# A convolution-and-experts block: another order of statistics and powers in phase 1, and normalisation and copies on other engines in phase 2

## The chip, the cores and the metric

The kernel runs on one core of a Trainium2 chip. Its engines are TensorE (PE, matmuls; PEld are its weight loads), VectorE (DVE), ScalarE (ACT), GpSimd (POOL) and the DMA queues of SyncE (SP) and GpSimd. Each engine executes its own instructions in program order, and engines wait for each other through semaphores. The metric is the device time of one execution in microseconds (us). PEclk is the TensorE clock that was granted, as a share of full speed; it has two levels, 1.0 (2.4 GHz) and 0.5 (1.2 GHz).

## The reference

```python
x = x + conv(ln_c(x))          # x: 16 x 56 x 56 tokens of 96 channels, f32
t = t + ffn(ln_t(t))           # t: the same 50,176 tokens

def conv(x):                   # 7x7 windows, 49 steps each
    w = ln(x, ln1_w, ln1_b)
    h[k] = w[k] @ Bm + h[k-1] @ A;   xr = h @ Cm
    return xr + gelu(ln(xr, ln2_w, ln2_b) @ W1 + b1) @ W2 + b2

def ffn(x):                    # 4 experts, the best 2 are kept
    probs = softmax(x @ gate_w + gate_b)
    masked = probs * top2mask / (sum(kept probs) + 1e-9)
    return sum_e masked[e] * (gelu(x @ w1[e] + b1[e]) @ w2[e] + b2[e])
```

The reciprocal standard deviations of the normalisations are the powers (var + eps) ** -0.5, and the softmax needs e ** (score - best score). Both are computed on GpSimd.

## The kernel before

**Phase 1** (the function `periods`, 49 tiles of 1,024 tokens) computes the convolution part of all tokens, the gate scores and the position of each token in a list sorted by its pair of experts, and scatters the rows to HBM by indirect DMAs of GpSimd (`scatter`, line 451, 8 for a tile). The tiles are the 49 steps of the recurrence; each has two halves of 512 tokens. Work on several tiles is interleaved in a period p. With r = p + 1, a period holds:

- TensorE: six `up` units (three 512-column matmuls each, lines 1040 to 1042) and six `down` units (line 1051; units 0 and 3 begin with line 1048, which must wait until VectorE has emptied the bank `tok_ps`) of tile p; `from_state(r)` (line 1075), `from_input(p+3)` (line 1060), transposes `turn_h(p+2)` and `turn_xr(r)` (line 1030), and two tiny `rank` matmuls of tile p-1 (lines 1114 and 1115), which need the finished gate of VectorE.
- VectorE: `take_state`, statistics of the input (`x_in`), of the recurrent rows (`xr`) and of the result rows (line 703 and 707, then `variance`, line 714), `gate`, `shift` (line 854), `add_x2` (lines 739 and 742, which empty `tok_ps`), `positions`, the sum `x_xr` (line 863) and `y_low` (line 754), the low part of a split into two fp32r numbers.
- GpSimd: per period one power of 16 columns (`powers_of_variance`, line 437, for `x_in` of tile p+4 and `xr` of tile r together), one of 8 columns (`rstd_t`, line 442) and the scatters.
- ScalarE: six gelus (line 569), `copy_xr` (line 545), `scale_in` (line 530, and the gate columns in line 533), `normalise_xr` (line 554, needs `shift`), `copy_h` (line 538) and `y_high` (line 562), in this order at a period's end: `normalise_xr(r,0)`, `copy_h` twice, `normalise_xr(r,1)`, `gelu(p,5)`, `scale_in(p+3,1)`, `y_high(r,0)`; `y_high(p,1)` opens the next period.

The chain that leads into the next period is thus: `from_state`, `copy_xr`, statistics, variance, power, `shift`, `normalise_xr`, transposes, `y_high`, `y_low`, first `up`. Regions of PSUM are guarded by `Region.take`: a matmul that writes one waits for the semaphore of its last reader. The input products and the rank matmuls share the region `inp`.

**Phase 2** takes 103 blocks of 512 sorted rows, of one pair of experts each. A block has 6 units u (3 for either expert); unit n = 6b + u has `up2(n)` and `down2(n)` on TensorE (lines 1160 to 1162 and 1174 to 1176), `gelu2` and `part_hi` on ScalarE (lines 610 and 616) and `part_lo` on VectorE (line 915). In step u the engines issue `up2(n+3)`, `gelu2(n+3)`, `part_hi(n+3)`, `part_lo(n+3)` and `down2(n)`. After three units the expert's result y lies in a PSUM bank; `copy_y2` copies it with the bias to SBUF (ScalarE, line 628), TensorE transposes it back (`turn_y2`, line 1183: that of the first expert in step 3, that of the second in step 1 of the next block), and VectorE adds it, weighted, to the rows (`combine`, line 969). VectorE computes the two weights of each row in step 2 (`weights`, lines 928 to 941) from the powers of GpSimd (`powers`, line 474), and `numbers` (line 957) gives the indices. GpSimd issues for each block the powers of the next one and four indirect DMAs that store the result (line 485). `normalise(b+2)` (line 950, VectorE, step 3) makes the normalised rows of a later block, `turn_t` (line 1146) transposes them in step 0, and `t_hi` and `t_lo` split them.

## Time and profile before

| | us |
|---|---|
| median of 3 runs | 2251.65 (2246.73 to 2255.51) |
| the profiled execution | 2249.75, span 2248.0 |
| phase 1, first `up` of tile 0 to first `up` of tile 48 (48 periods) | 65.0 to 1101.0 |
| handover: last tile, table of blocks, first rows | 1101.0 to 1146.2 |
| phase 2, to the end of the last block but for its stores | 1146.2 to 2234.3 |

Busy shares over the span are 90% for PE, 73% for PEld, 70% for DVE, 65% for ACT and 70% for POOL. They are averages over two phases with different limits. The granted clock of TensorE is 0.88 in phase 1 and 0.99 in phase 2. The page's shares of the chain that ended last are 39% POOL, 24% issue, 21% PE and 9% DVE. A timeline row gives the start, the duration, the engine, the line, the operation with out<-in, the shapes and the count, and in brackets the idle time of the engine ahead of it and what ended it; the start of the next row tells how soon the engine went on, since instructions overlap.

### The profile page before, as it was taken

To read this page: it belongs to the slowest core of one execution; us is meant where nothing else is said; L and a number is where in the kernel's file an instruction comes from. 1 tells how busy PE (TensorE), PEld (TensorE's weight loads), DVE (VectorE), ACT (ScalarE), POOL (GpSimd) and SP (SyncE) were. 2 spreads that over 40 slices of the span, in tenths; PEclk is the share of its full clock that TensorE was granted. 3 is DMA by queue.
4 is the path that set the end of the run, shared out by engine and by line. 5 is a ranking of instruction groups with operands and counts; after the bars stand their busy time and mean duration, and the time that the engine had idled before them with its cause. 6 is when DMAs were issued, how large, how long until landed. Compare 5 with 4: busy or idle time off the path is not lost.

```text
span 2248.0 us, 41456 instructions
## 1 busy us (share of the span) xinstructions
PE 2013.8 (90%) x10865; PEld 1643.5 (73%) x10865; DVE 1583.5 (70%) x7089; ACT 1461.7 (65%) x3019; POOL 1581.4 (70%) x1147
## 2 busy tenths in 40 slices
PE   4899999999999898889759999999999999999996
PEld 3788888888888788778637676676676666666664
DVE  5576666666676776676548777777777777777775
ACT  1555555454555555555338888888888888888885
POOL 2265555565555655655638888888898888988887
PEclk9988888888899999999869999999999999999998
DMA  5112122121212212221045555655556556555552
GB/s 156 45 51 60 50 62 58 52 64 46 64 46 64 65 48 64 57 61 29 25 138 177 175 175 166 178 167 171 176 163 178 173 167 178 166 177 174 165 180 68
DMA packets 120249, 251.68 MB, mean 112 GB/s; under 512 B 26689, under 2 KB 43707, under 8 KB 120016
## 3 DMA queue, kind: packets, MB, share of 16 engines
q1 hardware_dynamic: 91168, 207.24, 32.1%
q0 software_dynamic: 25728, 40.00, 5.5%
q10 hardware_dynamic: 3120, 1.80, 0.3%
q8 instruction: 89, 1.46, 0.3%
q14 instruction: 144, 1.18, 0.2%
HBM read 203.91 MB, written 46.00 MB: 111 GB/s over the span
## 4 chain that ended last, share of the span: by engine, by line
POOL 39%; issue 24%; PE 21%; DVE 9%; ACT 3%; another core or an unknown queue 1%; DMA 1%; SPq 1%; POOLq 0%; ACTq 0%; DVEq 0%
POOL out L485 27%; PE tok_ps L1051 7%; POOL rstd L437 6%; POOL ex L474 4%; PE turn_ps L1030 3%; DVE stats L703 3%; PE y_ps L1060 3%; PE mix_ps L1075 2%; POOL sorted_rows L451 2%; DVE moment L707 2%; PE up_ps L1040 1%; PE up_ps L1042 1%; PE up_ps L1041 1%; DVE h_tok L726 1%
## 5 line engine op out<-in xcount | busy, mean ns | idle before, releaser
L485 POOL DMA_INDIRECT out<-out_sb,idx x412 | 613.6, 1489 | 135.8 <-issue 112.4
L451 POOL DMA_INDIRECT sorted_rows<-rows,pos x392 | 384.9, 982 | 110.6 <-issue 108.4
L915 DVE TENSOR_TENSOR g_lo<-g,g_hi 128x512 fp32r<-128x512 f32 x618 | 398.2, 685 | 13.3 <-ACT g_hi L616 12.7
L616 ACT CAST g_hi<-g 128x512 fp32r<-128x512 f32 x618 | 382.2, 618 | 13.1
L1051 PE MATMUL tok_ps<-d_mlp,g 128*128 128x100 f32 x2352 | 360.5, 303 | 3.1 <-issue 3.1
L1051 PEld LDWEIGHTS tok_ps<-d_mlp,g 128*128 128x128 f32 x2352 | 336.9, 219 | 24.5 <-issue 23.5
L474 POOL TENSOR_TENSOR ex<-euler,rows 128x8 f32<-128x8 f32 x206 | 339.7, 1664 | 11.0 <-DMA rows<-sorted_rows 9.8
L569 ACT ACTIVATE g<-up_ps 128x512 f32<-128x512 f32 x294 | 172.9, 596 | 218.5 <-PE up_ps L1042 208.3
L1174 PE MATMUL mix_ps<-g_hi,ew 128*96 128x512 f32 x618 | 252.8, 409 | 65.8 <-issue 35.9
L437 POOL TENSOR_TENSOR rstd<-var_eps,neg_half 128x16 f32<-128x16 f32 x52 | 157.1, 3022 | 163.2 <-issue 97.6
L442 POOL TENSOR_TENSOR rows<-var_eps,neg_half 128x8 f32<-128x8 f32 x49 | 82.3, 1679 | 236.2 <-DVE var_eps L714 236.2
L1175 PE MATMUL mix_ps<-g_hi,ew 128*96 128x512 f32 x618 | 244.3, 395 | 0.0
L1176 PE MATMUL mix_ps<-g_lo,ew 128*96 128x512 f32 x618 | 243.7, 394 | 0.0
L754 DVE TENSOR_TENSOR y_lo<-turn_ps,y_hi 96x512 fp32r<-96x512 f32 x98 | 67.1, 686 | 243.3 <-issue 126.8
L628 ACT ACTIVATE y_sb<-mix_ps,ew 96x512 f32<-96x512 f32 x206 | 141.3, 686 | 112.6 <-PE mix_ps L1176 99.0
L554 ACT ACTIVATE xr_n<-xr,shift,rstd 128x96 f32<-128x96 f32 x392 | 151.8, 462 | 84.7 <-DVE shift L854 84.7
L610 ACT ACTIVATE g<-turn_ps 128x512 f32<-128x512 f32 x310 | 185.2, 597 | 32.5 <-PE turn_ps L1162 19.6
L610 ACT ACTIVATE g<-up_ps 128x512 f32<-128x512 f32 x308 | 183.5, 596 | 33.1 <-PE up_ps L1162 20.8
L1174 PEld LDWEIGHTS mix_ps<-g_hi,ew 128*96 128x96 f32 x618 | 99.5, 161 | 132.6 <-issue 59.5
L928 DVE TENSOR_TENSOR both<-ex,pair_of 128x32 f32<-128x32 f32 x103 | 19.8, 192 | 207.8 <-POOL ex L474 207.8
L1075 PE MATMUL mix_ps<-state_aug,h_t 97*128 97x196 f32 x800 | 156.1, 339 | 2.0 <-DVE gate_sum L731 1.4
L1060 PEld LDWEIGHTS y_ps<-in_w,x_t 96*128 96x128 f32 x784 | 138.0, 250 | 21.2 <-ACT gate_sum L533 6.4
(177 smaller groups left out, 4490.6 us busy)
## 6 DMA issues: line engine op xcount, KB each, us to landing
ew<-expert_w SPq DMA_DIRECT2D x206, 384.0 KB
ew<-expert_w SPq DMA_DIRECT2D x206, 288.5 KB
rows<-sorted_rows SPq DMA_DIRECT2D x103, 206.0 KB
x_in<-in_x SPq DMA_DIRECT2D x49, 384.0 KB
x_t<-in_x_chan SPq DMA_DIRECT2D x49, 384.0 KB
out<-out_sb,idx POOLq DMA_INDIRECT x412
sorted_rows<-rows,pos POOLq DMA_INDIRECT x392
sorted_rows<-pad_rows SPq DMA_DIRECT2D x11, 206.0 KB, 11.8
```

Source lines behind the costliest of these rows:

```text
L437: pool.tensor_tensor(rstd[:, n % 2, :, :], var_eps[:, LN_X:LN_T, :], neg_half[:, :].rearrange("p (k s) -> p k s", k=2), ALU.pow).then_inc( ...
L451: pool.indirect_dma_start(out=sorted_rows[:, :], out_offset=bass.IndirectOffsetOnAxis(ap=pos[:, r, s:s + 1], axis=0), in_=rows[:, r, s, :] ...
L474: pool.tensor_tensor(ex[:, b % 2, s:s + 2, :], euler[:, :].rearrange("p (s e) -> p s e", s=2), rows2[:, b % IN_RING, s:s + 2, COL_BELOW:CO ...
L485: pool.indirect_dma_start(out=out_rows, out_offset=bass.IndirectOffsetOnAxis(ap=idx[:, r, s:s + 1], axis=0), in_=out_sb[:, r, s, :], in_of ...
L610: act.activation(g[:, n % G_RING, :], up_bank(n), ACT.Gelu).then_inc(gelu2_done, 1)
L616: act.copy(g_hi[:, n % PART_RING, :], g[:, n % G_RING, :]).then_inc(hi_done, 1)
L915: dve.tensor_tensor(g_lo[:, n % PART_RING, :], g[:, n % G_RING, :], f(g_hi[:, n % PART_RING, :]), ALU.subtract).then_inc(lo_done, 1)
L1051: ins = pe.matmul(mlp_ps[:, s, :], g[:, n % G_RING, sub(s)], d_mlp[:, k, :], start=False, stop=(k == KB - 1 and s == HALF_SUBS - 1))
L1060: ins = pe.matmul(in_ps[:, s, :], x_t[:, t % XT_RING, sub(HALF_SUBS * h + s)], in_w[:, :], start=True, stop=True)
L1174: pe.matmul(y2_bank(q), hi, g_hi[:, part, :], start=(k == 0), stop=False)
L1175: pe.matmul(y2_bank(q), lo, g_hi[:, part, :], start=False, stop=False)
L1176: pe.matmul(y2_bank(q), hi, g_lo[:, part, :], start=False, stop=(k == KB - 1)).then_inc(down2_done, 1)
```

## The change

In phase 1, GpSimd computes one 16-column power for `x_in` of tile p+3 and the result rows of tile p-1 (`rstd_tokens`) and one of 8 columns for `xr` of tile r (`rstd_of_xr`), between scatters 0 and 1 and scatters 2 to 7 of tile p-2. VectorE takes both halves of the state with their statistics first, moves the statistics of the input to the end of the period, cuts `gate` in two (`gate_compares`, `gate_pairs`), and does `add_x2(p,0)` between them, ahead of `shift`; `positions` runs one period later, and the sum `x_xr` is made in halves (`add_xr`). Both `y_high` and both `y_low` stand at the end of a period. TensorE does the rank matmuls after the last transposes, ahead of `down(p,5)`. The scattered row holds -mean * rstd in place of the mean.

In phase 2, ScalarE normalises rows (`normalise`, four ACTIVATEs after `part_hi(6b+7)`, in step 4) and VectorE copies y with its bias (`copy_y2`, at the start of step 3, and for the second expert of step 0 of the next block). GpSimd computes one power of 16 columns for a block in place of two of 8. TensorE's order in phase 2 is as before.

```diff
-            def powers_of_variance(tx, tr):
-
-                n = rstd_calls(tx, tr)
+            def rstd_tokens(tx):
+
+                n, tt = token_power(tx), tx - 4
+                if tile(tt):
+                    pool.wait_ge(var_ok[LN_T], tt + 1)
                 if tile(tx):
                     pool.wait_ge(var_ok[LN_X], tx + 1)
-                if tile(tr):
-                    pool.wait_ge(var_ok[LN_R], tr + 1)
                 if tile(tx - 2):
                     pool.wait_ge(x_b_ok, 2 * (tx - 2) + 2)
-                if tile(tr - 2):
-                    pool.wait_ge(xr_n_ok, 2 * (tr - 2) + 2)
-                pool.tensor_tensor(rstd[:, n % 2, :, :], var_eps[:, LN_X:LN_T, :], neg_half[:, :].rearrange("p (k s) -> p k s", k=2),
+                if tile(tt - 2):
+                    pool.wait_ge(id_ok, tt - 1)
+                pool.tensor_tensor(rstd[:, n % 2, :, :], var_eps[:, LN_T:LN_R, :], neg_half[:, :].rearrange("p (k s) -> p k s", k=2),
                                    ALU.pow).then_inc(rstd_ok, 1)
 
-            def rstd_t(t):
-                pool.wait_ge(var_ok[LN_T], t + 1)
-                pool.tensor_tensor(rows[:, t % ROW_RING, :, COL_RSTD], var_eps[:, LN_T, :], neg_half[:, 0:SUBS],
-                                   ALU.pow).then_inc(rstd_t_ok, 1)
+            def rstd_of_xr(t):
+                pool.wait_ge(var_ok[LN_R], t + 1)
+                if t >= 2:
+                    pool.wait_ge(xr_n_ok, 2 * (t - 2) + 2)
+                pool.tensor_tensor(rstd_r[:, t % 2, :], var_eps[:, LN_R, :], neg_half[:, 0:SUBS], ALU.pow).then_inc(rstd_r_ok, 1)
...
             for p in periods():
+                if tile(p + 3) or tile(p - 1):
+                    rstd_tokens(p + 3)
                 if tile(p - 2):
-                    scatter(p - 2, (1,))
-                if tile(p - 1):
-                    rstd_t(p - 1)
+                    scatter(p - 2, (0, 1))
+                if tile(p + 1):
+                    rstd_of_xr(p + 1)
                 if tile(p - 2):
-                    scatter(p - 2, (2, 3))
-                if tile(p + 4) or tile(p + 1):
-                    powers_of_variance(p + 4, p + 1)
-                if tile(p - 2):
-                    scatter(p - 2, (4, 5, 6, 7))
-                if tile(p - 1):
-                    scatter(p - 1, (0,))
+                    scatter(p - 2, (2, 3, 4, 5, 6, 7))
 
             def powers(b):
                 pool.wait_ge(rows_loaded[b % IN_RING], 16 * (b // IN_RING + 1))
                 if b >= 2:
                     pool.wait_ge(weight_step, 6 * (b - 2) + 2)
-                for s in range(0, BSUBS, 2):
-                    pool.tensor_tensor(ex[:, b % 2, s:s + 2, :], euler[:, :].rearrange("p (s e) -> p s e", s=2),
-                                       rows2[:, b % IN_RING, s:s + 2, COL_BELOW:COL_MEAN], ALU.pow).then_inc(ex_ok, 1)
+                pool.tensor_tensor(ex[:, b % 2, :, :], euler[:, :].rearrange("p (s e) -> p s e", s=BSUBS),
+                                   rows2[:, b % IN_RING, :, COL_BELOW:COL_SHIFT], ALU.pow).then_inc(ex_ok, 1)
...
             for p in periods():
                 r = p + 1
                 if tile(p):
-                    y_high(p, 1)
                     gelu(p, 0)
                     gelu(p, 1)
                 if tile(r):
...
                 if tile(r):
                     y_high(r, 0)
+                    y_high(r, 1)
...
+            def normalise(b):
+                act.wait_ge(rows_loaded[b % IN_RING], 16 * (b // IN_RING + 1))
+                if b >= 2:
+                    act.wait_ge(t_turned, b - 1)
+                for s in range(BSUBS):
+                    row = rows2[:, b % IN_RING, s, :]
+                    ins = act.activation(t_tok[:, b % 2, s, :], row[:, COL_X2:COL_BELOW], ACT.Identity,
+                                         scale=row[:, COL_RSTD:COL_ID], bias=row[:, COL_SHIFT:COL_RSTD])
+                ins.then_inc(t_tok_ok, 1)
+
+            normalise(0)
             t_hi(0)
             for n in range(AHEAD):
                 gelu2(n)
                 part_hi(n)
+            normalise(1)
             for b in range(BLOCKS):
                 for u in range(UNITS):
                     n = UNITS * b + u
                     if n + AHEAD < UNITS * BLOCKS:
                         gelu2(n + AHEAD)
-                    if u % KB == KB - 1:
-                        copy_y2(n // KB)
                     if n + AHEAD < UNITS * BLOCKS:
                         part_hi(n + AHEAD)
+                    if u == 4 and b + 2 < BLOCKS:
+                        normalise(b + 2)
                     if u == 0 and b + 1 < BLOCKS:
                         t_hi(b + 1)
...
+            def add_xr(t, h):
+                subs = slice(HALF_SUBS * h, HALF_SUBS * (h + 1))
+                if t >= 2:
+                    dve.wait_ge(x2_ok, 2 * (t - 2) + h + 1)
+                dve.tensor_tensor(x_xr[:, t % 2, subs, :], xr[:, subs, :], x_in[:, t % X_RING, subs, :], ALU.add).then_inc(x_xr_ok, 1)
...
-            def gate(t):
+            def gate_compares(t):
...
+            def gate_pairs(t):
...
             for p in periods():
                 r = p + 1
-                if tile(p):
-                    y_low(p, 1)
                 if tile(p - 1):
                     add_x2(p - 1, 1)
                     rows_stats(p - 1, 1)
-                    variance(LN_T, p - 1, (rstd_t_ok, p - 1))
+                    variance(LN_T, p - 1, (rstd_ok, token_power(p + 2) + 1))
+                if tile(p - 2):
+                    positions(p - 2)
                 if tile(r) or r == -1:
                     take_state(r, 0)
+                if tile(r):
+                    xr_stats(r, 0)
+                    add_xr(r, 0)
+                if tile(r) or r == -1:
+                    take_state(r, 1)
+                if tile(r):
+                    xr_stats(r, 1)
+                    variance(LN_R, r, (rstd_r_ok, r))
+                if tile(p - 1):
+                    gate_compares(p - 1)
+                if tile(p):
+                    add_x2(p, 0)
+                if tile(r):
+                    dve.wait_ge(rstd_r_ok, r + 1)
+                    if r >= 1:
+                        dve.wait_ge(xr_n_ok, 2 * (r - 1) + 2)
+                    dve.scalar_tensor_tensor(shift[:, :], in0=moment[:, LN_R, :, 0], scalar=-1.0, in1=rstd_r[:, r % 2, :],
+                                             op0=ALU.mult, op1=ALU.mult).then_inc(shift_ok, 1)
+                if tile(p - 1):
+                    gate_pairs(p - 1)
+                if tile(r):
+                    add_xr(r, 1)
+                if tile(p):
+                    rows_stats(p, 0)
                 if tile(p + 4):
                     t = p + 4
                     dve.wait_ge(x_loaded[t % X_RING], 16 * (t // X_RING + 1))
                     for h in range(2):
                         half_stats(LN_X, t, h, x_in[:, t % X_RING, :, :])
-                    variance(LN_X, t, (rstd_ok, rstd_calls(t - 1, t - 4) + 1))
+                    variance(LN_X, t, (rstd_ok, token_power(t - 1) + 1))
...
                 if tile(r):
-                    xr_stats(r, 0)
-                if tile(r) or r == -1:
-                    take_state(r, 1)
-                if tile(r):
-                    xr_stats(r, 1)
-                    variance(LN_R, r, (rstd_ok, rstd_calls(r + 2, r - 1) + 1))
-                if tile(p - 1):
-                    gate(p - 1)
-                if tile(r):
-                    n = rstd_calls(r + 3, r)
-                    dve.wait_ge(rstd_ok, n + 1)
-                    if r >= 1:
-                        dve.wait_ge(xr_n_ok, 2 * (r - 1) + 2)
-                    dve.scalar_tensor_tensor(shift[:, :], in0=moment[:, LN_R, :, 0], scalar=-1.0, in1=rstd[:, n % 2, LN_R, :],
-                                             op0=ALU.mult, op1=ALU.mult).then_inc(shift_ok, 1)
-                if tile(p):
-                    add_x2(p, 0)
-                if tile(p - 1):
-                    positions(p - 1)
-                if tile(r):
-                    if r >= 2:
-                        dve.wait_ge(x2_ok, 2 * (r - 1))
-                    dve.tensor_tensor(x_xr[:, r % 2, :, :], xr[:, :, :], x_in[:, r % X_RING, :, :], ALU.add).then_inc(x_xr_ok, 1)
-                if tile(p):
-                    rows_stats(p, 0)
-                if tile(r):
                     y_low(r, 0)
+                    y_low(r, 1)
...
-            def normalise(b):
...
+            def copy_y2(q):
+                dve.wait_ge(down2_done, KB * (q + 1))
+                if q >= 2:
+                    dve.wait_ge(y2_turned, q - 1)
+                dve.tensor_scalar(y_sb[:, q % 2, :], y2_bank(q), f(ew[0:C, q % EW_RING, E_B2:E_B2 + 1]), None, ALU.add).then_inc(
+                    y2_copied, 1)
...
             for b in range(BLOCKS):
                 for u in range(UNITS):
                     n = UNITS * b + u
+                    if u == 0 and b >= 1:
+                        copy_y2(2 * b - 1)
+                    if u == 3:
+                        copy_y2(2 * b)
                     if u == 1 and b >= 1:
                         combine(2 * b - 1)
                     if u == 2:
@@ -996,8 +1010,7 @@
                         part_lo(n + AHEAD)
                     if u == 0 and b + 1 < BLOCKS:
                         t_lo(b + 1)
-                    if u == 3 and b + 2 < BLOCKS:
-                        normalise(b + 2)
+            copy_y2(2 * BLOCKS - 1)
...
                     turn_h(p + 2, 1)
+                if tile(p + 3):
+                    from_input(p + 3, 1)
+                if tile(p):
+                    down(p, 3)
+                    up(p, 5)
+                if tile(r):
+                    turn_xr(r, 0)
+                if tile(p):
+                    down(p, 4)
+                if tile(r):
+                    turn_xr(r, 1)
                 if tile(p - 1):
                     inp.take(pe, base_set, p)
                     pe.wait_ge(score_counted, p)
                     pe.matmul(rank_ps[:, 0:TYPES], earlier[:, :], count[:, :, SUBS - 1], start=True, stop=True)
                     pe.matmul(rank_ps[:, TYPES:2 * TYPES], ones[:, :], count[:, :, SUBS - 1], start=True, stop=True).then_inc(
                         ranked, 1)
-                if tile(p):
-                    down(p, 3)
-                    up(p, 5)
-                if tile(p + 3):
-                    from_input(p + 3, 1)
-                if tile(r):
-                    turn_xr(r, 0)
-                if tile(p):
-                    down(p, 4)
-                if tile(r):
-                    turn_xr(r, 1)
                 if tile(p):
                     down(p, 5)```

VectorE in phase 1, from the variance of `xr` (the second half of its statistics is just done) to the emptying of `tok_ps`, before:

```order
L714 TENSOR_SCALAR var_eps<-moment 128x8
L763 TENSOR_TENSOR score<-gate_sum,rows 128x32
...
L780 TENSOR_TENSOR rows<-score,top 128x8x4
L783 TENSOR_REDUCE rank<-beaten 128x32
L785 TENSOR_SCALAR kept<-rank 128x32
...
L797 SCALAR_TENSOR_TENSOR count<-restart,of_pair 128x48
L854 SCALAR_TENSOR_TENSOR shift<-moment,rstd 128x8
L739 TENSOR_TENSOR rows<-tok_ps,x_xr 128x4x96
L742 TENSOR_TENSOR gate_sum<-tok_ps,gate_sum 128x16
```

and the same place in the changed kernel:

```order
L715 TENSOR_SCALAR var_eps<-moment 128x8
L771 TENSOR_TENSOR score<-gate_sum,rstd 128x32
...
L784 TENSOR_TENSOR beaten<-score 128x8x3
L740 TENSOR_TENSOR rows<-tok_ps,x_xr 128x4x96
L743 TENSOR_TENSOR gate_sum<-tok_ps,gate_sum 128x16
L861 SCALAR_TENSOR_TENSOR shift<-moment,rstd_r 128x8
L796 TENSOR_TENSOR rows<-score,top 128x8x4
L799 TENSOR_REDUCE rank<-beaten 128x32
```

The emptying of `tok_ps` has moved ahead of `shift`, and the second half of the gate behind it.

VectorE in phase 2, from the index copy of step 2 of one block to the first weight instruction of the next, before:

```order
L957 CAST idx<-rows 128x4
L915 TENSOR_TENSOR g_lo<-g,g_hi 128x512 x2
L950 TENSOR_SCALAR t_tok<-rows 128x96 x4
L969 SCALAR_TENSOR_TENSOR out_sb<-tok_ps,weight,rows 128x96 x4
L915 TENSOR_TENSOR g_lo<-g,g_hi 128x512 x3
L920 TENSOR_TENSOR y_lo<-y_ps,y_hi 96x512
L969 SCALAR_TENSOR_TENSOR out_sb<-tok_ps,weight,out_sb 128x96 x4
L915 TENSOR_TENSOR g_lo<-g,g_hi 128x512
L928 TENSOR_TENSOR both<-ex,pair_of 128x32
```

and in the changed kernel:

```order
L962 CAST idx<-rows 128x4
L930 TENSOR_TENSOR g_lo<-g,g_hi 128x512
L968 TENSOR_SCALAR y_sb<-mix_ps,ew 96x512
L930 TENSOR_TENSOR g_lo<-g,g_hi 128x512
L981 SCALAR_TENSOR_TENSOR out_sb<-tok_ps,weight,rows 128x96 x4
L930 TENSOR_TENSOR g_lo<-g,g_hi 128x512 x2
L968 TENSOR_SCALAR y_sb<-mix_ps,ew 96x512
L930 TENSOR_TENSOR g_lo<-g,g_hi 128x512
L935 TENSOR_TENSOR y_lo<-y_ps,y_hi 96x512
L981 SCALAR_TENSOR_TENSOR out_sb<-tok_ps,weight,out_sb 128x96 x4
L930 TENSOR_TENSOR g_lo<-g,g_hi 128x512
L943 TENSOR_TENSOR both<-ex,pair_of 128x32
```

The four `t_tok` rows are gone, and a copy of y (`y_sb<-mix_ps,ew`) stands behind the first `g_lo` after the weights and another ahead of the last but one.

## Rows read from the trace of the kernel before

**Rows 1.** Windows: stretch, busy (x) of PE, PEld, DVE, ACT, POOL, PEclk, DMA.
```profile
65.00:1101.00 1036.00, 951.36 (x5717) 853.92 (x5717) 690.43 (x4089) 549.63 (x1419) 585.96 (x465) 0.88 0.19 53
...
1146.20:2234.30 1088.10, 1013.09 (x4944) 749.61 (x4944) 844.23 (x2783) 891.24 (x1545) 949.34 (x614) 0.99 0.57 169
594.74:618.35 23.61, 22.27 (x122) 20.11 (x121) 15.07 (x88) 11.74 (x30) 12.52 (x10) 0.78 0.19 52
704.25:723.65 19.40, 17.70 (x123) 15.77 (x122) 14.49 (x87) 10.93 (x29) 11.86 (x10) 1.00 0.20 47
```

**Rows 2.** Timeline of TensorE in phase 1, in the tile that begins at 704.25.
```profile
709.21 1.49 PE L1075 MATMUL mix_ps<-state_aug,h_t 97*128 97x196 f32 x8
...
716.17 0.36 PE L1114 MATMUL y_ps<-count,earlier 128*128 128x6 f32 x2 [0.52 <-DVE count L797]
...
717.60 0.44 PE L1048 MATMUL tok_ps<-b_parts,ones_r 2*128 2x400 f32 x1 [0.85 <-DVE gate_sum L742]
```

**Rows 3.** Timeline of VectorE in phase 1, the next tile.
```profile
732.64 0.53 DVE L726 TENSOR_TENSOR h_tok<-mix_ps,x_b 128x384 f32<-128x384 f32 x1
...
734.34 0.17 DVE L714 TENSOR_SCALAR var_eps<-moment 128x8 f32<-128x8 f32 x1
...
735.52 0.19 DVE L780 TENSOR_TENSOR rows<-score,top 128x32 f32<-128x32 f32 x1
...
737.70 0.17 DVE L854 SCALAR_TENSOR_TENSOR shift<-moment,rstd 128x8 f32<-128x8 f32 x1 [0.78 <-POOL rstd L437]
...
743.80 0.69 DVE L754 TENSOR_TENSOR y_lo<-turn_ps,y_hi 96x512 fp32r<-96x512 f32 x1 [2.33 <-ACT y_hi L562]
```

**Rows 4.** Timeline of GpSimd in phase 1, the same tile.
```profile
728.81 1.68 POOL L442 TENSOR_TENSOR rows<-var_eps,neg_half 128x8 f32<-128x8 f32 x1 [4.50 <-DVE var_eps L714]
...
734.65 3.01 POOL L437 TENSOR_TENSOR rstd<-var_eps,neg_half 128x16 f32<-128x16 f32 x1 [1.67 <-issue]
```

**Rows 5.** Timeline of ScalarE in phase 1, the same tile.
```profile
725.48 0.58 ACT L562 CAST y_hi<-turn_ps 96x512 fp32r<-96x512 f32 x1 [2.60 <-remote]
...
731.12 0.48 ACT L545 COPY xr<-mix_ps 128x384 f32<-128x384 f32 x1 [0.87 <-PE mix_ps L1075]
...
737.90 1.55 ACT L554 ACTIVATE xr_n<-xr,shift,rstd 128x96 f32<-128x96 f32 x4 [2.10 <-DVE shift L854]
...
743.17 0.60 ACT L562 CAST y_hi<-turn_ps 96x512 fp32r<-96x512 f32 x1
```

**Rows 6.** Timeline of GpSimd in phase 2, one block.
```profile
1599.76 3.29 POOL L474 TENSOR_TENSOR ex<-euler,rows 128x8 f32<-128x8 f32 x2
...
1607.53 2.65 POOL L485 DMA_INDIRECT out<-out_sb,idx  x1 [0.30 <-issue]
1610.18 3.30 POOL L474 TENSOR_TENSOR ex<-euler,rows 128x8 f32<-128x8 f32 x2
```

**Rows 7.** Waits from 1200 to 2200 us: engine, line, waited for, us, times, longest.
```profile
DVE both L928 <- POOL ex L474: 200.6, 96, 2.1
```

**Rows 8.** Timeline of VectorE in an early block of phase 2.
```profile
1174.00 1.00 DVE L969 SCALAR_TENSOR_TENSOR out_sb<-tok_ps,weight,out_sb 128x96 f32<-128x96 f32 x4
...
1175.51 0.19 DVE L928 TENSOR_TENSOR both<-ex,pair_of 128x32 f32<-128x32 f32 x1
...
1176.79 0.69 DVE L915 TENSOR_TENSOR g_lo<-g,g_hi 128x512 fp32r<-128x512 f32 x1
```

**Rows 9.** Timeline of TensorE there: steps 1 and 3, then step 1 again.
```profile
1173.40 0.49 PE L1183 MATMUL tok_ps<-ident,y_sb 96*128 96x96 f32 x4
...
1176.57 0.49 PE L1183 MATMUL tok_ps<-ident,y_sb 96*128 96x96 f32 x4
...
1182.97 0.49 PE L1183 MATMUL tok_ps<-ident,y_sb 96*128 96x96 f32 x4
```

**Rows 10.** Timeline of ScalarE there: the first gelu after the second transposes, and its high part.
```profile
1177.83 0.60 ACT L610 ACTIVATE g<-turn_ps 128x512 f32<-128x512 f32 x1
1178.46 0.63 ACT L616 CAST g_hi<-g 128x512 fp32r<-128x512 f32 x1
```

62 lines of the change are left out of this document (26 added, 36 removed).

## The prediction

> **What bounds the kernel now.** I read the windows first, because the busy shares of the page average two phases with different limits. Phase 1 takes 1036 us for 48 periods, 21.58 each, at a granted clock of 0.88; phase 2 takes 1088 at 0.99 [rows 1]. These two are 94% of the span, so each is priced by itself.
>
> In phase 1 TensorE sets the time, together with its clock. The tile that begins at 704.25 runs at full clock and takes 19.40; the one at 594.74 has a granted clock of 0.78 and takes 23.61 [rows 1]. In the first, TensorE waits twice: 0.52 for the finished gate ahead of the rank matmuls, and 0.85 for the emptying of `tok_ps` ahead of `down(p,3)` [rows 2]. Both waits recur in every tile, and most of them are followed by a stretch at half clock. Without the two waits a tile at full clock has 19.40 - 1.37 = 18.03 of work. The second wait comes from `add_x2`, which stands behind `shift` on VectorE, and `shift` waits for the power of 3.01 us on GpSimd [rows 3, 4].
>
> In phase 2 the waits name GpSimd: VectorE waits 200.6 us, 96 times, for the powers [rows 7]. From one pair of powers to the next pass 10.42 us, and GpSimd goes straight from the last store into the next power [rows 6]. A block is therefore 10.42, although TensorE can do one in 9.57: in an early block, where GpSimd is not yet behind, the same transposes recur after 1182.97 - 1173.40 [rows 9].
>
> **Phase 1, part by part.** Times are counted from the first `up` of a tile at full clock. The second `from_state` ends at 709.21 + 1.49 - 704.25 = 6.45 [rows 2], and the copy of `xr` starts at 6.50 and takes 0.48 [rows 5]. Now the statistics of the input stand in front of what follows on VectorE; they go to the end of the period. So `h_tok` starts at 7.00, the variance 1.70 later (734.34 - 732.64, [rows 3]) and ends at 8.87. The power has 8 columns, which took 1.68, in place of 16 with 3.01 [rows 4]: with 0.1 for the handing over it ends at 10.65, and `shift` starts at 10.70. Beside the power VectorE has the compares (735.52 - 734.34 = 1.18, and 0.1 for one more instruction) and `add_x2` (about 0.55), which fit. `tok_ps` is then empty well before `down(p,3)`, and the rank matmuls stand four units later than the gate needs: both waits go.
>
> What is late next? From `shift` to `y_low` pass 743.80 - 737.70 = 6.10, to the first `up` another 0.69 and 0.06 [rows 3]: the next tile could start at 17.55. ScalarE has `gelu(p,4)` just ahead of `normalise_xr` then, 0.3 more: 17.85. A new wait appears: the rank matmuls share the region `inp` with `from_input(p+3,1)`, so they wait for the last gate columns of ScalarE, copied just ahead of `y_high`, which starts 5.47 after `shift` [rows 5], that is at about 16.5. That leaves 1.5 for rank and `down(p,5)` until 18.0. Chain and work meet: I take 18.03. The power of 16 columns is now for other rows and has several us of slack; the scatters (some 1.27 each) end before the next one is asked for. Cutting `x_xr` in two and one more small instruction cost 0.2 on VectorE, which still has slack ahead of `take_state`. `positions` (about 1.1) fits ahead of the state, which arrives 3.1 after the period's start.
>
> Sum: 48 x (21.58 - 18.03) = 170 less. ScalarE has nine waits of about 2.60 with no releaser in the trace, one of them at 725.48 [rows 5]; the chain has no slack for these, so 9 x 2.6 = 23 comes back: **-147**. If the clock still falls in part of the tiles, a tile costs 19 to 19.5 and the gain is 100; without the 23 it is 170.
>
> **Phase 2, part by part.** GpSimd gains: one power of 16 columns (3.01, [rows 4]) for two of 8 (3.29, [rows 6]), 0.3 a block. That would be the whole story if GpSimd stayed the bound. But `copy_y2` has moved into VectorE's order, behind `combine`, the weights and two `g_lo`, while TensorE's `turn_y2` of step 3 still stands where it stood, ahead of every further `up2`. The loop, from the start of that transposition:
>
> - TensorE transposes, does `up2(6b+7)`, ScalarE its gelu and high part: in the early block from 1176.57 to the start of `g_hi` at 1178.46 [rows 9, 10], 1.89; ScalarE goes on 0.52 later, 2.41.
> - `normalise(b+2)` now stands here. Its nearest row is `xr_n`, four ACTIVATEs of 96 columns out of SBUF with scale and bias per row: 1.55, 1.45 to the next start [rows 5]. On VectorE it took less, but the row to go by is ScalarE's own. 3.86.
> - Gelu and high part of unit 6b+8: 1178.46 + 0.63 - 1177.83 = 1.26 [rows 10]. 5.12, and 0.02 to VectorE.
> - VectorE: `g_lo` 0.60, copy of y 0.66, `g_lo` 0.60, `y_lo` 0.60, `combine` and `g_lo` 1.51 (1175.51 - 1174.00), weights and indices 1.28 (1176.79 - 1175.51), `g_lo` 0.60 [rows 8], copy of y until done 0.74, and 0.06 to TensorE. 5.14 + 6.65 = 11.79.
>
> The trace of before has no copy of y on VectorE; its nearest row is `y_lo`, 96x512 from PSUM, 0.69 [rows 3], and I add 0.05 for the pointer operand (bounds 0.60 and 0.80, so the loop is 11.6 to 11.9). So a block takes **11.79 in place of 10.42**, whatever GpSimd does: +1.37 over 102 blocks is +140. In the early block one sees the same thing: TensorE reaches its transposes of step 3 at 1176.57, when VectorE is still at the weights (until 1176.79), behind which come `g_lo` and then the copy [rows 8, 9].
>
> TensorE then stands still for 11.79 - 9.57 = 2.2 in one piece in every block. In phase 1 waits of 0.52 and 0.85 close together were enough to bring half clock in most tiles [rows 1, 2]. At half clock the transposes and the `up2` at the loop's head (about 1.2) double: +1.2 if that happens in each block, 0 if in none. I take one block in three, +0.4: in phase 2 TensorE is otherwise denser than in phase 1. Sum: (1.37 + 0.4) x 102 = **+180**.
>
> A rule of the Trainium skill bears on ScalarE's new part ("VectorE: DVE Perf Modes", the section on the TRN2 errata): instructions with SBUF sources pay a fixed extra latency each, and ScalarE takes 224 cycles and one per element. Four pieces of 96 columns would be 1.07 us by it, an estimate, and the sum 39 us lower; here the trace's 1.55 is used.
>
> The handover between the phases has the 3.01 power in place of 1.68 and else the same chain: 0 to 3, taken as 0.
>
> **Sum.** 2249.75 (profiled execution; the median is 1.9 higher) - 147 + 180 = **2283**.
>
> **Rivals.**
> 1. The loop holds, but the clock does not fall in phase 2, and phase 1 gets its 147 to 170: 2249.75 - 147 + 140 = 2243, down to 2220. For it: phase 2 is at 0.99 now, with a wait of TensorE in every block. This ends on the fast side where phase 1 gains over 150. Chance 0.28.
> 2. VectorE, freed of its wait of 2.1 for the powers [rows 7], runs ahead far enough, and the copy is never late: TensorE's 9.57 decides, 2249.75 - 147 - 0.85 x 102 = 2016; with GpSimd as the bound at 10.1 it is 2070. Against it stands the loop, in which GpSimd has no part. The Trainium skill supports half of it ("SBUF — State Buffer", Who interferes with whom): a `tensor_scalar` between fp32 tiles in SBUF locks GpSimd out of its port while it makes descriptors, and the `t_tok` rows are such; without them the stores would be shorter. The store of 2.65 [rows 6] starts after them and lies beside `g_lo`, so the trace does not bear the rule out for the longest store. Chance 0.08.
> 3. The clock falls after the wait in nearly each block: 2249.75 - 147 + 2.57 x 102 = 2365. It decides where half clock follows more than two thirds of the waits. Chance 0.14.
> 4. Phase 1 keeps half of its half-clock stretches, because the rank matmuls' new wait (0.5) is followed by little work: 2249.75 - 100 + 180 = 2330. Chance 0.14.
>
> **How the numbers follow.** My forecast, 2262 to 2310 with 2283 in it, has 0.36, of which 0.07 lies within 0.5%. A measurement of this kernel can tell 0.5% (11 us) from no change. Faster by more: 0.19 of rival 1 and 0.08 of rival 2, 0.27. Within: 0.09 of rival 1 and 0.07, 0.16. Slower: 0.57. The range takes in rival 1 with the short loop (2205) and most of rivals 3 and 4 (2380); rival 2 and the worst of rival 3 are left out.
>
> **What would show it.** In the changed profile: no wait ahead of `tok_ps` in phase 1, a wait ahead of the rank matmuls of about 0.5, a period of about 18.0 to 18.6 and a clock near 1.0 there. In phase 2: a wait of about 2 us of TensorE ahead of the transposes of `y_sb` once per block, none of VectorE for the powers, GpSimd waiting for `combine`, and a block of 11.8 to 12.2. A block under 10.42 would refute the loop; a period over 20 the phase 1 part.

## The result

The changed kernel takes **2429.7 us** (2419.9 to 2467.5) beside 2250.4 of the kernel before: a ratio of 1.077, interval 1.073 to 1.082. Slower was right, but 2283 was forecast, in a range up to 2380. Later runs on other chips showed that both kernels take different times there. The record does not name the chip of the result; it is called A here.

| chip | before | changed kernel | ratio [interval] |
|---|---|---|---|
| A (the result) | 2250.4 | 2429.7 | 1.077 [1.073, 1.082] |
| B | 2248.3 | 2377.9 | 1.059 [1.055, 1.063] |
| F | 2177.0 | 2260.1 | 1.037 [1.033, 1.040] |

The execution profiled with the result (2467.5) was a slow one, 45 above the median of the others (2422.5) and left out of the ratio, so the profile of after is read from the run of the unchanged kernel on chip B (`a0_after`), beside the one on chip F (`g0_after`). The windows are phase 1 (first to last `up`) and phase 2 (first to last transposition of y), for the kernel before, the changed kernel on B, and the changed kernel on F. Columns: stretch, busy us of PE, PEld, DVE, ACT, POOL, granted clock, DMA share, GB/s.

```profile
65.00:1110.30 1045.30, 960.57 (x5771) 861.43 (x5772) 697.29 (x4130) 552.62 (x1424) 591.52 (x470) 0.89 0.19 53
1167.00:2232.40 1065.40, 998.72 (x4904) 739.46 (x4902) 834.37 (x2754) 882.21 (x1531) 941.88 (x609) 1.00 0.57 169
```

```profile
68.60:1052.70 984.10, 906.50 (x5767) 795.21 (x5768) 704.69 (x4220) 540.70 (x1424) 599.53 (x467) 0.95 0.19 56
1110.70:2360.40 1249.70, 1073.88 (x4903) 780.46 (x4903) 894.99 (x2555) 911.20 (x1727) 746.91 (x509) 0.94 0.51 144
```

```profile
69.00:937.60 868.60, 852.88 (x5767) 759.51 (x5768) 699.94 (x4220) 539.49 (x1424) 602.29 (x467) 0.99 0.21 64
993.40:2244.50 1251.10, 1075.65 (x4903) 782.60 (x4903) 894.66 (x2554) 911.19 (x1727) 747.12 (x509) 0.94 0.51 144
```

Phase 2 is longer by 184, the same on both chips (1249.7 and 1251.1), and 180 was forecast. Phase 1 is the part that went wrong: on B it gained 61 in place of 147, and on F it is 116 shorter than on B with the same instructions. On A it gained about 17: the profiled execution has 1073.0 for phase 1, less the 45 by which it lay high, an estimate that puts all of the 45 there. Its phase 2 is 1248, no longer than on B, so the 45 do lie ahead of it.

**Phase 2 in the profile.** Transposes of y on TensorE (chip B), with the idle time ahead in brackets; these answer to [rows 9]:

```profile
1612.99 0.55 PE L1196 MATMUL tok_ps<-ident,y_sb 96*128 96x96 f32 x4 [1.46 <-DVE y_sb L968]
...
1619.57 0.55 PE L1196 MATMUL tok_ps<-ident,y_sb 96*128 96x96 f32 x4
...
1624.81 0.55 PE L1196 MATMUL tok_ps<-ident,y_sb 96*128 96x96 f32 x4 [1.88 <-DVE y_sb L968]
```

ScalarE and then VectorE in the same block, in answer to [rows 10] and [rows 8]:

```profile
1614.31 0.60 ACT L606 ACTIVATE g<-turn_ps 128x512 f32<-128x512 f32 x1 [2.20 <-PE turn_ps L1175]
...
1615.47 1.54 ACT L626 ACTIVATE t_tok<-rows 128x96 f32<-128x96 f32 x4
1616.91 0.58 ACT L606 ACTIVATE g<-up_ps 128x512 f32<-128x512 f32 x1
1617.52 0.62 ACT L612 CAST g_hi<-g 128x512 fp32r<-128x512 f32 x1
```

```profile
1618.17 0.69 DVE L930 TENSOR_TENSOR g_lo<-g,g_hi 128x512 fp32r<-128x512 f32 x1 [1.88 <-ACT g_hi L612]
1618.78 0.74 DVE L968 TENSOR_SCALAR y_sb<-mix_ps,ew 96x512 f32<-96x512 f32 x1
...
1622.14 0.18 DVE L943 TENSOR_TENSOR both<-ex,pair_of 128x32 f32<-128x32 f32 x1
...
1623.42 0.68 DVE L930 TENSOR_TENSOR g_lo<-g,g_hi 128x512 fp32r<-128x512 f32 x1
1624.02 0.74 DVE L968 TENSOR_SCALAR y_sb<-mix_ps,ew 96x512 f32<-96x512 f32 x1
```

This is the forecast loop. From the transposes at 1612.99 over ScalarE's rows to `g_lo` at 1618.17 pass 5.18 (5.14 forecast), and from there over `g_lo`, copy, `g_lo`, `y_lo`, `combine`, `g_lo`, weights, `g_lo` and copy to the next transposes 6.64 (6.65 forecast). VectorE has no wait for a power any more, and GpSimd waits for the combination:

```profile
POOL out L481 <- DVE out_sb L981: 343.1, 88, 5.0
```

The wait of TensorE brings half clock in part of the blocks. The block above, and the next one:

```profile
1612.99:1624.81 11.82, 9.94 (x48) 7.16 (x49) 8.70 (x26) 8.88 (x17) 7.48 (x6) 1.00 0.56 152
1624.81:1637.59 12.78, 11.29 (x49) 8.28 (x49) 8.91 (x26) 9.12 (x17) 7.04 (x6) 0.87 0.48 137
```

Of 101 blocks, 58 run at full clock with a mean of 11.81 and 43 have a stretch of half clock and a mean of 12.78: 0.97 more in 43%, or 0.41 a block.

**Phase 1 in the profile.** The same tile end on chip B and on chip F. First B: TensorE's transposes of `xr_n`, then ScalarE's `y_hi`, which reads them.

```profile
781.17 0.60 PE L1043 MATMUL turn_ps<-ident,xr_n 128*96 128x128 f32 x4
781.61 1.03 PE L1064 MATMUL tok_ps<-d_mlp,g 128*128 128x100 f32 x8
782.48 0.60 PE L1043 MATMUL turn_ps<-ident,xr_n 128*96 128x128 f32 x4
```

```profile
783.51 0.58 ACT L558 CAST y_hi<-turn_ps 96x512 fp32r<-96x512 f32 x1 [0.19 <-PE turn_ps L1043]
786.50 0.58 ACT L558 CAST y_hi<-turn_ps 96x512 fp32r<-96x512 f32 x1 [2.40 <-remote]
```

Then chip F:

```profile
713.91 0.60 PE L1043 MATMUL turn_ps<-ident,xr_n 128*96 128x128 f32 x4
...
715.22 0.60 PE L1043 MATMUL turn_ps<-ident,xr_n 128*96 128x128 f32 x4
```

```profile
715.92 1.08 ACT L558 CAST y_hi<-turn_ps 96x512 fp32r<-96x512 f32 x2
```

On F both casts run one behind the other as soon as the second transposes end at 715.82. On B the transposes end at 781.77 and 783.08 by their rows, but the second cast starts at 786.50, 3.4 later, and nothing else holds it: ScalarE is idle for 2.40. Of the two semaphores for which it waits, that of `up(5)` had risen by 781.35; that of the transposes changes at 783.49 and 786.47 in the trace. "remote" is what the profile says when a semaphore changed at a moment at which no instruction ended. In the text below this is a **late signal**. The waits of `y_hi` for them in phase 1, on B, and what follows on TensorE:

```profile
ACT y_hi L558 <- remote: 85.2, 42, 2.8
...
PE mix_ps L1088 <- DVE gate_sum L732: 32.4, 36, 1.2
```

On F there is no wait `<- remote` in phase 1, nor this wait of TensorE. There a tile takes 17.82 to 17.85 in 44 of 48 periods, where 18.03 was forecast. One caution goes with the word late: the profile models the ends of matmuls, so the rows cannot tell whether the signal lags behind the work or the work behind its row. What ScalarE waits for is real in either case.

### The profile page after: what moved, and what is told of

The parts are those of the page before. It is cut to its first block, busy times and chain, and to the rows that moved or that the text cites. A ratio compares the mean times of both kernels' runs of the same rounds, so it can differ in the third digit from the quotient of the medians.

```text
span 2465.7 us, 41499 instructions
## 1 busy us (share of the span) xinstructions
PE 2099.8 (85%) x10865; PEld 1673.4 (68%) x10865; DVE 1652.6 (67%) x6981; ACT 1490.6 (60%) x3225; POOL 1398.9 (57%) x1045
## 3 DMA queue, kind: packets, MB, share of 16 engines
q8 instruction: 89, 1.46, 0.3%
## 4 chain that ended last, share of the span: by engine, by line
issue 28%; DVE 22%; POOL 19%; PE 18%; ACT 8%; POOLq 1%; SPq 0%; DMA 0%; another core or an unknown queue 0%; ACTq 0%; DVEq 0%
POOL sorted_rows L452 13%; DVE g_lo L930 7%; DVE y_sb L968 5%; ACT t_tok L626 4%; DVE out_sb L981 4%; POOL rstd_r L444 3%; PE tok_ps L1196 3%; POOL rstd L437 2%; ACT g L606 2%; PE mix_ps L1187 2%; PE mix_ps L1188 2%; PE mix_ps L1189 2%; ACT g_hi L612 2%; PE turn_ps L1173 1%; PE up_ps L1173 1%
## 5 line engine op out<-in xcount | busy, mean ns | idle before, releaser
L481 POOL DMA_INDIRECT out<-out_sb,idx x412 | 421.1, 1022 | 515.4 <-DVE out_sb L981 406.8
L930 DVE TENSOR_TENSOR g_lo<-g,g_hi 128x512 fp32r<-128x512 f32 x618 | 422.9, 684 | 316.1 <-ACT g_hi L612 237.1
L612 ACT CAST g_hi<-g 128x512 fp32r<-128x512 f32 x618 | 383.0, 620 | 19.6
L565 ACT ACTIVATE g<-up_ps 128x512 f32<-128x512 f32 x294 | 174.1, 597 | 300.6 <-PE up_ps L1055 270.3
L1064 PE MATMUL tok_ps<-d_mlp,g 128*128 128x100 f32 x2352 | 344.5, 293 | 0.7 <-issue 0.5
L470 POOL TENSOR_TENSOR ex<-euler,rows 128x16 f32<-128x16 f32 x103 | 335.2, 3254 | 11.3 <-DMA rows<-sorted_rows 10.2
L1064 PEld LDWEIGHTS tok_ps<-d_mlp,g 128*128 128x128 f32 x2352 | 313.1, 205 | 23.4 <-issue 22.1
L437 POOL TENSOR_TENSOR rstd<-var_eps,neg_half 128x16 f32<-128x16 f32 x53 | 156.7, 2957 | 272.4 <-DVE var_eps L715 272.4
L606 ACT ACTIVATE g<-turn_ps 128x512 f32<-128x512 f32 x310 | 183.8, 593 | 161.5 <-PE turn_ps L1175 133.0
L606 ACT ACTIVATE g<-up_ps 128x512 f32<-128x512 f32 x308 | 182.6, 593 | 156.8 <-PE up_ps L1175 117.5
L1196 PE MATMUL tok_ps<-ident,y_sb 96*128 96x96 f32 x824 | 114.0, 262 | 177.2 <-DVE y_sb L968 166.5
L1196 PEld LDWEIGHTS tok_ps<-ident,y_sb 96*128 96x128 f32 x824 | 80.7, 143 | 258.5 <-DVE y_sb L968 238.1
L1088 PE MATMUL mix_ps<-state_aug,h_t 97*128 97x196 f32 x800 | 196.3, 401 | 13.3 <-DVE gate_sum L732 12.5
L1088 PEld LDWEIGHTS mix_ps<-state_aug,h_t 97*128 97x128 f32 x800 | 182.4, 244 | 32.3 <-issue 19.4
L1053 PE MATMUL up_ps<-y_hi,w_hi 98*128 98x512 f32 x294 | 158.2, 538 | 26.7 <-DVE y_lo L761 14.4
L626 ACT ACTIVATE t_tok<-rows 128x96 f32<-128x96 f32 x412 | 158.6, 456 | 36.6 <-DMA rows<-sorted_rows 36.6
L444 POOL TENSOR_TENSOR rstd_r<-var_eps,neg_half 128x8 f32<-128x8 f32 x49 | 83.3, 1701 | 148.4 <-DVE var_eps L715 148.4
```

What stands on the lines that cost most here:

```text
L470: pool.tensor_tensor(ex[:, b % 2, :, :], euler[:, :].rearrange("p (s e) -> p s e", s=BSUBS), rows2[:, b % IN_RING, :, COL_BELOW:COL_SHIFT] ...
L481: pool.indirect_dma_start(out=out_rows, out_offset=bass.IndirectOffsetOnAxis(ap=idx[:, r, s:s + 1], axis=0), in_=out_sb[:, r, s, :], in_of ...
L606: act.activation(g[:, n % G_RING, :], up_bank(n), ACT.Gelu).then_inc(gelu2_done, 1)
L612: act.copy(g_hi[:, n % PART_RING, :], g[:, n % G_RING, :]).then_inc(hi_done, 1)
L930: dve.tensor_tensor(g_lo[:, n % PART_RING, :], g[:, n % G_RING, :], f(g_hi[:, n % PART_RING, :]), ALU.subtract).then_inc(lo_done, 1)
L1064: ins = pe.matmul(mlp_ps[:, s, :], g[:, n % G_RING, sub(s)], d_mlp[:, k, :], start=False, stop=(k == KB - 1 and s == HALF_SUBS - 1))
```

## The experiments

P1 and P2 are the two stretches defined above. Runs on one chip were made together and share the runs of the kernel before.

| run | chip, before there | us | ratio [interval] | P1 | P2 |
|---|---|---|---|---|---|
| a0_after | B, 2248.3 | 2377.9 | 1.059 [1.055, 1.063] | 984 | 1250 |
| a1_old_phase2 | B | 2200.1 | 0.978 [0.976, 0.981] | 989 | 1069 |
| a4_new_phase2 | B | 2429.1 | 1.081 [1.076, 1.085] | 1037 | 1250 |
| a5_small_loads | B | 2373.5 | 1.057 [1.051, 1.062] | 979 | 1248 |
| a2_copy_on_scalar | C, 2244.8 | 2119.0 | 0.941 [0.935, 0.947] | 991 | 990 |
| a3_norm_on_vector | C | 2273.7 | 1.012 [1.007, 1.017] | 981 | 1150 |
| b5_later_turn | C | 2152.2 | 0.959 [0.953, 0.964] | 984 | 1025 |
| b1_scatters_spread | C | 2376.3 | 1.058 [1.053, 1.063] | 980 | 1249 |
| e1_pause | D, 2178.4 | 2042.1 | 0.936 [0.931, 0.942] | 913 | 988 |
| e2_swap | D | 2000.1 | 0.917 [0.911, 0.922] | 870 | 989 |
| e3_positions | D | 2009.3 | 0.921 [0.916, 0.927] | 881 | 989 |
| e4_swap_positions | D | 2011.6 | 0.923 [0.918, 0.928] | 880 | 988 |
| f0_base | E, 2176.0 | 1994.3 | 0.917 [0.913, 0.920] | 865 | 989 |
| f1_pause | E | 2045.9 | 0.940 [0.937, 0.944] | 912 | 988 |
| f2_swap | E | 1998.2 | 0.918 [0.915, 0.922] | 868 | 989 |
| f3_positions | E | 2009.8 | 0.923 [0.920, 0.927] | 882 | 989 |
| g0_after | F, 2177.0 | 2260.1 | 1.037 [1.033, 1.040] | 869 | 1251 |
| g1_pause | F | 2308.8 | 1.060 [1.056, 1.064] | 916 | 1249 |

### The parts, one by one

The theory was that the phases are independent; the rival that phase 1 had gained as forecast and lost it through phase 2.

> The changed kernel once more, as the control beside the other three: 2420 to 2435. From its profile the difference to the kernel before is to be split: phase 1 (first to last up) +10 to +30 where -147 was forecast, phase 2 about +180 as forecast, the handover under 5.

> New phase 1, old phase 2 (rows normalised on VectorE, y copied on ScalarE, two powers per block; the row holds the shift in place of the mean, so VectorE multiplies and adds). If the two parts add up and the new phase 1 is worth nothing: 2245 to 2285. If phase 1 is worth the 147 that I forecast and only lost it through phase 2 (the clock): 2100 to 2120.

> Old phase 1 (which writes the shift in place of the mean, one small instruction for another), new phase 2 whole. If the loop through the copy of y sets phase 2 alone: +165 to +190, 2415 to 2440, a block of 11.8 to 12.3, TensorE waiting 1.5 to 2 ahead of its transposes of y_sb. If part of the slowdown comes from phase 1: below 2400.

Old phase 2 takes 2200, new phase 2 on the old phase 1 takes 2429: -48 and +181 against the kernel before, and the two together are +133 where the whole change is +130. The parts add up; the rival is out. `a1_old_phase2` itself lies between its two forecasts (2245 to 2285 and 2100 to 2120): its P1 is 56 shorter than that of before, where nothing or 147 had been the alternatives. The block of the old phase 2 is 10.47 and VectorE waits for the powers as in [rows 7]: with two powers, GpSimd is the bound again. The forecasts for the control (2420 to 2435, P1 +10 to +30) missed: I had taken them from chip A, P1 from the disturbed execution there.

### Phase 2: which of its edits

`a2_copy_on_scalar` moves the copy of y back to ScalarE, between gelu and high part (ScalarE's order; in VectorE's the two calls go):

```diff
                         gelu2(n + AHEAD)
+                    if u % KB == KB - 1:
+                        copy_y2(n // KB)
```

> The changed kernel with the copy of y back on ScalarE (between gelu and high part, as before); rows still normalised on ScalarE, one power. The control took 2378 on the last chip and its phase 2 is 180 longer than the old one. If the forecast loop (the copy of y late on VectorE) is the cause: most of the 180 goes, and what is left is ScalarE's own work, 8.65 a block before and 1.5 more for the rows, so a block of 10.4 to 11.0 and 2200 to 2265. If the move of the rows to ScalarE is the cause: 2350 or more.

`a3_norm_on_vector` moves the normalising back (VectorE multiplies and adds the shift). The first two lines are ScalarE's order, the others VectorE's:

```diff
-                    if u == 4 and b + 2 < BLOCKS:
-                        normalise(b + 2)
+                    if u == 3 and b + 2 < BLOCKS:
+                        normalise(b + 2)
```

> The changed kernel with the normalising of the rows back on VectorE; the copy of y still on VectorE, one power. The forecast loop loses its 1.45 of ScalarE and would be 10.3: a block of 10.3 to 10.8 and 2200 to 2260. If the copy's place alone is what costs, whatever ScalarE does beside it: 2330 or more.

`b5_later_turn` leaves all work on its engine and moves two calls by a step, first in TensorE's order, then in VectorE's:

```diff
-                    if u == 3:
+                    if u == 4:
                         turn_y2(2 * b)
...
-                    if u == 4:
+                    if u == 5:
                         combine(2 * b)
```

> The changed kernel with TensorE's first transposition of y in a block one step later (step 4 in place of 3) and the combination that reads it one step later too (5 in place of 4); all work stays on its engine. If TensorE's order closes the loop, the copy now has 1.6 more and is never late: TensorE's wait of 1.5 to 2 goes, a block of 10.1 to 11.0, 2200 to 2290. If an engine is simply full (ScalarE or VectorE), nothing changes: 2365 to 2390.

The loop is confirmed, by the run that moves no work above all: with the transposition a step later a block takes 10.0 in place of 11.8, no block has half clock, and the time is below the forecast of 2200 to 2290. TensorE's idle time ahead of the transposes of y falls to 0.3 a block. The copy back on ScalarE gives 9.67 (P2 shorter by 260, 80 under the kernel before). That was better than I had expected (10.4 to 11.0). I had added 1.5 of ScalarE per block to its 8.65; in a window of one block it is busy for 9.53, and the whole block is bound by TensorE:

```profile
606.10:623.93 17.83, 17.54 (x123) 15.68 (x122) 14.73 (x90) 11.27 (x30) 12.81 (x11) 1.00 0.25 70
1612.00:1621.66 9.66, 9.66 (x50) 7.24 (x49) 7.30 (x23) 9.53 (x21) 7.06 (x6) 1.00 0.60 175
```

(These are a tile and a block of the same kernel on chip E.) The normalising back on VectorE gives 11.22; I had expected 10.3 to 10.8. Taking 1.45 out of the loop shortened it by only 0.6: TensorE still waits, 1.48 in the block that follows.

```profile
1599.93 0.55 PE L1196 MATMUL tok_ps<-ident,y_sb 96*128 96x96 f32 x4 [1.48 <-DVE y_sb L964]
...
1611.16 0.55 PE L1196 MATMUL tok_ps<-ident,y_sb 96*128 96x96 f32 x4 [1.48 <-DVE y_sb L964]
```

The rows that VectorE now normalises itself (1600.40 to 1601.41) are not what is left, since VectorE waits twice behind them:

```profile
1603.93 0.69 DVE L916 TENSOR_TENSOR g_lo<-g,g_hi 128x512 fp32r<-128x512 f32 x1 [0.70 <-ACT g_hi L612]
...
1606.98 0.99 DVE L977 SCALAR_TENSOR_TENSOR out_sb<-tok_ps,weight,out_sb 128x96 f32<-128x96 f32 x4 [0.37 <-PE tok_ps L1196]
```

From the transposes at 1599.93 to this `g_lo` pass 4.00, where 5.18 less 1.44 would be 3.74: ScalarE, freed of the rows, now waits for TensorE's next `up2`. From there to the next transposes pass 7.23 in place of 6.64, most of it because `combine` has caught up with TensorE's transposes of step 1 and waits for them. Other waits took the place of the rows.

So it is the copy behind `combine`, weights and `g_lo` on VectorE, together with TensorE's fixed place for the transposes, that costs; the rows on ScalarE add to it. The same trace bears on a page that the prediction weighed ("SBUF — State Buffer", Who interferes with whom, in the Trainium skill). VectorE's `t_tok` is a `tensor_scalar` between fp32 tiles in SBUF, and a store of GpSimd runs beside it. The first row is VectorE's, the second GpSimd's, which starts 0.03 earlier:

```profile
1611.63 1.09 DVE L951 TENSOR_SCALAR t_tok<-rows 128x96 f32<-128x96 f32 x4
```

```profile
1611.60 1.04 POOL L481 DMA_INDIRECT out<-out_sb,idx  x1 [0.30 <-issue]
```

It takes 1.04, as stores do elsewhere (a mean of 1.04 in this kernel, 1.03 with the rows on ScalarE). Stores that start while such an instruction already runs are in the trace of before: there are 100, and they take 1.01 on average and 1.03 at most. So here the page's rule has no price that shows. The mean store of 1.49 belongs to the two kernels with two powers in a block (before, `a1_old_phase2`); what makes their fourth store 2.65 long [rows 6] was not tried.

### Phase 1: where the signals are late

Two suspects stand beside the late signals in the trace of chip B: the burst of the loads of x, and the train of GpSimd's scatters, whose last one starts 1.9 before the signals come, in tile after tile.

`a5_small_loads` lets every load of x beyond the first of each ring move an eighth of its bytes (the edit shown, and the same for the turned copy of x):

```diff
+                n = TOK // P * C if t < X_RING else C
-                sp.dma_start(x_in[:, t % X_RING, :, :].rearrange("p s c -> p (s c)"), x[t, :, :]).then_inc(
+                sp.dma_start(x_in[:, t % X_RING, :, :].rearrange("p s c -> p (s c)")[:, 0:n], x[t, :, 0:n]).then_inc(
```

> The changed kernel, but all loads of x after the first ones of each ring move an eighth of their bytes (an eighth of the columns; the rest of the buffers keeps old rows, so the result is not the reference's). In the changed profile ScalarE waits 1.3 and then 1.0 ahead of y_hi in nearly each tile, for completion signals of TensorE's transposes that come up to 3 us after the transposes' recorded end, and this falls together with the burst of the two loads of x. If the loads hold the signals back: these waits go, a tile takes 18.0 to 19.0, phase 1 is 100 to 150 shorter and the time 2270 to 2330. If the signals are late for another reason (scatters, instruction fetch, TensorE itself being behind its records): within 15 of the control.

`b1_scatters_spread` issues three of a tile's eight scatters one period later, where GpSimd was idle:

```diff
+                if tile(p - 3):
+                    scatter(p - 3, (5, 6, 7))
                 if tile(p + 3) or tile(p - 1):
                     rstd_tokens(p + 3)
...
-                    scatter(p - 2, (2, 3, 4, 5, 6, 7))
+                    scatter(p - 2, (2, 3, 4))
+            scatter(TILES - 1, (5, 6, 7))
```

> The changed kernel, but the last three of a tile's eight scatters are issued one period later, ahead of the power, where GpSimd was idle for 4.3. In the control TensorE's completion signals of the end of a tile come up to 3.8 late, all at one moment that lies 1.92 to 1.95 after the start of the last scatter of the train, whatever else stands there, and the small loads of the run before changed nothing. If the train of scatters holds the signals back: ScalarE's waits ahead of y_hi (85 in all) shrink to under 30, tiles take 18.0 to 18.6 as they now do where no scatter is in flight, and the time falls by 60 to 110, to 2270 to 2320. If scatters hold back signals wherever they are, the delay moves to the start of the tile: within 20 of the control. If they have no part in it: the same waits ahead of y_hi.

Neither changed anything. The waits of `y_hi`, with small loads (chip B, 85.2 in the control) and then with the scatters spread (chip C, where the three other kernels with this phase 1 have 79.8 to 81.8):

```profile
ACT y_hi L560 <- remote: 79.2, 43, 2.8
```

```profile
ACT y_hi L561 <- remote: 84.6, 40, 2.8
```

Neither the bytes of the loads nor the length of the train makes the signals late; the constant distance to the last scatter is that of a schedule in which everything is in step. What is left is something about TensorE itself, or about what carries its signals. The rows spoke for a row of short instructions: at the end of a tile some forty matmuls follow each other 0.11 apart, and in the four tiles of chip B with the most half clock no signal of these transposes is late. The first row is one of the four. The second row, a tile at full clock right behind another of them, has these signals 1.7 and 3.4 late again, though it takes only 18.12:

```profile
124.33:150.11 25.78, 24.27 (x123) 21.56 (x122) 15.16 (x90) 11.72 (x31) 12.83 (x11) 0.74 0.17 50
603.70:621.82 18.12, 17.52 (x123) 15.67 (x122) 14.53 (x89) 10.90 (x29) 12.34 (x10) 1.00 0.24 65
```

To test this I took `a2_copy_on_scalar` as base and made three edits: a pause of TensorE, an order in which `up(5)` breaks the row, and the positions out of the way of `h_tok`. The pause (TensorE; `g1_pause` has it on the changed kernel itself):

```diff
+                    if tile(p):
+                        pe.wait_ge(gelu_done, UNITS * (p + 1))
                     turn_xr(r, 0)
```

The swap (TensorE):

```diff
                     down(p, 3)
-                    up(p, 5)
                 if tile(r):
                     turn_xr(r, 0)
                 if tile(p):
+                    up(p, 5)
                     down(p, 4)
```

The positions (VectorE; `e4_swap_positions` has both this edit and the swap):

```diff
-                if tile(p - 2):
-                    positions(p - 2)
                 if tile(r) or r == -1:
                     take_state(r, 0)
...
                     add_xr(r, 0)
+                if tile(p - 2):
+                    positions(p - 2)
```

> Base: the changed kernel with the copy of y on ScalarE (2119, phase 1 991). One wait added on TensorE and no work: ahead of the first transposes of xr_n it waits for the gelu of unit 5, which comes about 1.0 later than it now starts them. If TensorE's completion signals are late because too many short instructions (0.11 apart) come in a row without a pause (they are late only at the end of that row, and not in tiles in which TensorE runs at half clock): the pause lets them catch up, ScalarE's waits ahead of y_hi for late signals (82 in all) nearly go, and phase 1 gets no longer, or shorter: 930 to 995, 2060 to 2125. If the signals are late for a reason outside TensorE: the pause comes on top, phase 1 1010 to 1045, 2140 to 2175.

> The same base; in TensorE's order the first transposes of xr_n stand ahead of up(5) in place of behind it, so the three long matmuls of up(5) break the row of short ones and the signal for y_hi has less in front of it. Row theory: the signal of the first transposes comes on time, the waits ahead of y_hi fall to 20 to 50, a tile takes 19 to 19.6, phase 1 910 to 960, 2040 to 2090. Cause outside TensorE: the release at the end of the row stays where it is, phase 1 980 to 995, 2110 to 2125.

> The same base; on VectorE the positions of tile p-2 stand behind the first half of h_tok, its gate columns, statistics and x + xr, in place of ahead of them. TensorE now waits 33 in all (34 times about 1.0) ahead of the second from_state for those gate columns. If it is the positions that are in the way: these waits go and phase 1 is 30 to 50 shorter, 2070 to 2090. If the next wait takes their place (the scatters start 1.2 later, and so does the power for the shift behind two of them): phase 1 980 to 1000, 2110 to 2130.

> Both edits together, to see whether they add up: if they do and each works, phase 1 870 to 930, 2000 to 2060; if the tile is then bound by something else, no better than the better of the two.

These four seemed to confirm everything: no late signal in any, and P1 between 870 and 913 where it had been 991. But all four gained, even the one whose edit had nothing to do with TensorE's order, and the kernel before took 2178 on that chip in place of 2245. Without a control there the runs told nothing, so the base ran beside three of them on one chip, E, where the kernel before again took 2176.

> The changed kernel with the copy of y on ScalarE, as control of the next three. If this chip gives late completion signals as the first ones did: about 2119, phase 1 990, 80 of ScalarE's waits for late signals. If it is like the last chip (before at 2178): few or no late signals, phase 1 880 to 930 and about 2010 to 2050, since then the forecast 18.0 per tile and 0.7 to 1.0 of wait behind the positions decide.

> The pause of TensorE ahead of the transposes of xr_n once more, now beside its control. With late signals on this chip: phase 1 no longer than the control's if the row of short instructions makes them late, 20 to 50 longer if the cause lies outside TensorE. Without late signals: 10 to 40 longer than the control (the pause costs 1.1 in each tile).

> The transposes of xr_n ahead of up(5), beside the control. With late signals: phase 1 30 to 80 shorter by the row theory, within 10 by the other. Without them: 10 to 40 shorter, since y_hi comes 0.7 earlier in the chain that sets the tile.

> The positions behind h_tok on VectorE, beside the control: TensorE's wait of about 1.0 ahead of the second from_state goes; 20 to 50 shorter if nothing takes its place, within 10 if late signals or the later scatters do.

On chip E the untouched base has no late signal either, and with 865 it is the shortest of the four. So the gain on D was not the edits'. What the edits do where no signal is late is now plain. The pause costs 47. TensorE is idle for 39 more: its own wait is 53.5, and the 13.3 ahead of the rank matmuls are gone. The rest is longer busy time, at a granted clock of 0.98.

```profile
PE turn_ps L1040 <- ACT g L565: 53.5, 48, 2.5
```

The swap costs 3, and the positions behind `h_tok` cost 18. The wait that the last edit was to remove is not there on this chip, and TensorE's wait ahead of the rank matmuls doubles, from the first line (base) to the second:

```profile
PE y_ps L1135 <- ACT gate_sum L529: 13.3, 45, 0.6
```

```profile
PE y_ps L1135 <- ACT gate_sum L529: 26.6, 45, 0.7
```

All three forecasts for a chip without late signals missed: 10 to 40 longer for the pause, 10 to 40 shorter for the swap, and for the positions 20 to 50 shorter or a change within 10.

The last two runs put the changed kernel itself on one chip with the pause. The chip, F, turned out to be of the kind without late signals.

> The changed kernel, unchanged. On a chip without late signals (before at 2176): phase 1 865, phase 2 1250, 2245 to 2260, so 3 to 4% slower than the kernel before. On one with late signals (before at 2248): 2370 to 2430, phase 1 980 to 1030.

> The changed kernel with TensorE's wait for the gelu of unit 5 ahead of the transposes of xr_n. Without late signals the pause costs what it did: phase 1 912, 47 longer than the control. With late signals: phase 1 910 to 985 and not over the control's if the row of short instructions makes them late; 20 to 50 longer than the control if the cause lies outside TensorE.

The sum for this kind of chip, 2245 to 2260, was made ahead of the run; it took 2260.1. The pause costs 47 again, as forecast. **What remains open** is why TensorE's signals are late on A, B and C and never on D, E and F, and whether a pause would cure it where they are: the pause only ever ran where there was nothing to cure. That they come from a row of short instructions is an inference from the rows, not shown.

The traces themselves hold another suspect. Traces of the same kernel have the same number of instructions, but not of recorded semaphore changes: 20,819 for `a2_copy_on_scalar` on C, and 32,715 for `f0_base`, the same kernel on E. All traces of A, B and C have 20,563 to 22,920, all of D, E and F 32,565 to 32,715. So about a third of these records is missing exactly where signals are late, for VectorE and ScalarE as well as for TensorE, and in phase 2 too, whose time is the same on both kinds. Whether the recording of a trace holds the signals back on A, B and C, or whether both have a common cause, no run tells. If it does, the 3% between the chips are the recording's and not the program's.

## Why the prediction was wrong

**Phase 2, the loop: right.** 11.79 was forecast for a block at full clock, and 11.81 is its mean. The copy was taken at 0.74 until done, between bounds of 0.60 and 0.80, and measures 0.74. The rows on ScalarE were taken at 1.45 from start to start, by [rows 5], and take 1.44 (1615.47 to 1616.91). The estimate from the Trainium skill's page ("VectorE: DVE Perf Modes", TRN2 errata), 1.07, did not hold; the row did.

**Phase 2, the clock: right in size.** Forecast was +1.2 in one block of three, 0.4 on average; measured is +0.97 in 43 of 101, 0.41. Together +180 forecast and +184 measured. Rival 1 (no fall of the clock) and rival 3 (a fall in nearly each block) are out, and so is rival 2: VectorE did not run ahead. The 8-column powers joined into one are worth nothing as long as the loop stands, as forecast. With the loop gone they may be worth something: the block of 9.67 has one power, that of 10.47 (`a1_old_phase2`) two, but those kernels differ in the rows' engine too, so this was not isolated.

**The handover: right.** From the last `up` to the first transposition of y pass 56.7 before (1110.3 to 1167.0) and 58.1 after. A term that I had not named is the first `up`, 3.6 later (68.6 for 65.0).

**Phase 1, the chain: right where its conditions hold.** "A tile at full clock, 18.03" is 17.85 on F in nearly every tile, and 17.9 and 18.3 in the two tiles of B that have full clock and no late signal. No wait stands ahead of `tok_ps` on F but for three; the wait ahead of the rank matmuls, forecast at about 0.5, is 13.0 in 45 tiles, 0.3 each:

```profile
PE y_ps L1138 <- ACT gate_sum L529: 13.0, 45, 0.6
```

**Phase 1, the term that failed** is "ScalarE has nine waits of about 2.60 with no releaser in the trace ... so 9 x 2.6 = 23 comes back". I counted these waits as a fixed price of nine events. They were the visible part of signals that are late at the end of many tiles: in the trace of before the second half's transposes signal over 0.3 late in about half of the tiles, but ScalarE's casts wait for a late signal only 9 times (22.8). The rest seems to have lain beside other work (argued from the order, not tried), since the second `y_high` stood in the next period. The change puts both `y_high` into the period's end, on the chain without slack that I had worked out myself, so that nearly every tile pays. On B ScalarE waits 85.2, in 42 waits, and TensorE, which is thrown out of step by it, waits for `h_tok` and `tok_ps` behind the positions too. Together with half clock behind those waits this is how I read the 116 between B (984) and F (869), two chips with one kernel: 62 of it is TensorE's idle time (77.6 against 15.7 in the windows), 54 is longer busy time of the same instructions (906.5 against 852.9).

**The clock in phase 1** went with it. "The clock near 1.0" is true on F (0.99) and half true on B (0.95, with tiles like the one of 25.78 at 0.74). Rival 4 had the right sign, half clock that stays in phase 1, but the wrong cause: on F the rank matmuls' wait is there in every tile and the clock does not fall behind it.

**The reference point.** The 147 were counted from a profile in which late signals and half clock made a period 21.58 long. On D, E and F the kernel before takes 72 less. Phase 2 is the same on every chip to 2 us in the kernels that ran on two (990 and 989, 1250 and 1251), so the 72 lie in phase 1: 973 in place of 1045, an estimate. There the new phase 1 gains 973 - 869 = 104. With about 4 for the later first `up` and the handover, -104 + 184 + 4 = +84 stands beside +83 on F, and -17 + 184 + 4 = 171 beside 172 on A (2422.5 less 2250.4). These two sums show only that the parts were added up rightly, since the 104 and the 17 were themselves taken from totals. On B all terms are read from traces: -61 + 184 + 5 = 128, beside 130 between the medians.

So the step that failed is the price of the late signals: 23 was put on them, as if their number stayed. On B, where the waits grew to 85.2, phase 1 gained 61 in place of 147; where no signal is late it gained 104, an estimate, since the 21.58 from which the gain was counted was itself a period with late signals. Why they are late stays open.

**The range.** It was built from mechanisms inside the program. That the same program has two speeds by the chip it runs on was not in it, and a range of 2205 to 2380 holds B (2378) and F (2260), but not A.

**A version that beats both.** The changed kernel with only the copy of y back on ScalarE takes 2119 (0.941 of before) on chip C and 1994 (0.917) on E. On E TensorE bounds both phases in it: idle for 0.29 of a tile of 17.83, and for nothing of a block of 9.66, by the windows above. So the change held a gain of 6% (C) to 8% (E), and one of its moves gave it back.

## What to carry to other kernels

When a copy moves to another engine, follow the loop from the consumer's fixed place in its own order back to that place: here the place of one transposition in TensorE's order turned two cheap edits into 1.4 a block, and moving that call by one step gave 1.8 back. A wait that the profile ascribes to nobody is not a constant: ask what would happen if it fell in every round of the loop, before a change takes the slack from behind it. And never read an edit's effect without the control on the same chip: four edits "gained" 78 to 121 in phase 1 here, where the untouched base gained as much.

## What the runs showed of the hardware that I had not expected

- Completion signals of TensorE can come long after its rows end (the profile models these ends): after the second transposes of `xr_n` by up to 3.8, in a burst with those of the work behind them, and over 0.3 late in 39 to 45 of 49 tiles with the new phase 1 on chips A, B and C. On D, E and F the greatest delay there is 0.01.
- On the same three chips the traces lack about a third of the semaphore changes (20,563 to 22,920, beside 32,565 to 32,715 on D, E and F).
- The late signals do not depend on the bytes of the loads in flight (an eighth: 79.2 of waits in place of 85.2) nor on the length of the train of scatters (84.6).
- The same kernel differs by 3% between chips (2248 and 2176), and a kernel with less slack by 5 to 7% (2378 and 2430 against 2260), while the phase with long matmuls differs by 0.1%.
- Pauses of TensorE of 0.3 in each tile leave the clock at 1.0 in 47 of 48 tiles (`g0_after`); a pause of 1.5 to 1.9 in each block brings half clock in 43% of them in one kernel (`a0_after`) and in 1 of 101 in another with 1.48 (`a3_norm_on_vector`).
